# ScalarE takes the key's exponential first, and VectorE puts gate and key row between its two normalisations

## The chip, the cores and the metric

One core of one Trainium2 chip runs the whole program in one launch. The metric is the device time of that launch in microseconds (us). Five engines work side by side, each through an instruction list of its own, and meet at semaphores: TensorE (PE, with its weight loads shown as PEld), VectorE (DVE), ScalarE (ACT), GpSimd (POOL) and SyncE (SP), which issues transfers.

## The reference, cut to what matters

A pre-norm block: attention, then a mixture of experts. The change is in the attention part, which for each of 8 sequences of 512 tokens, 16 query heads and 4 key heads adds a causal softmax attention and a gated linear attention:

```python
q, k, v = x @ Wq, x @ Wk, x @ Wv                  # 16 / 4 / 4 heads of 128; g = k
qs = softmax(q, axis=-1); ks = softmax(k, axis=-1)  # over the 128 features of a head
gl = log_sigmoid(k) / 16.0
sq, sk = rotary(q), rotary(k)
# linear part, a scan over tokens:
S = S * exp(g_t)[..., None] + k_t[..., None] * v_t[..., None, :]   # k_t from ks, g_t from gl
o_gla = einsum('bhk,bhkv->bhv', q_t, S)                            # q_t from qs
# softmax part:
y = softmax(causal(sq @ sk.T * D ** -0.5)) @ v
out = (0.5 * y + 0.5 * o_gla) @ Wo
```

## The kernel before

The attention phase works in units: one unit is one key head with its four query heads of one sequence, so there are 32. While a unit c is attended, the features of unit c + 1 are prepared, in the same instruction lists. A unit has four steps s = 0 to 3. In step s each engine does, interleaved and in an order written out by hand:

- for the attended unit, head s: the scores of its four query blocks i = 3, 2, 1, 0, each with a row maximum (`row_max`, DVE), an exponential with row sum (`exponent`, ACT), a normalisation (`normalise`: a reciprocal of the row sum and a multiplication of `prob`, DVE), a transposition on PE (`turn_probs`), and the copy of the transposed blocks to `prob_t` (`past` on ACT, `diagonal` on DVE); then PE's `attend` and ACT's two output copies (`out_copy`), whose low part POOL makes (`out_low`). Scores, maxima, exponentials and normalisations of blocks 3 and 2 of head s + 1 are already done in step s.
- for the prepared unit, token tile a (a counts all 128 tiles, s is the tile within a unit): ACT takes the products from PSUM (`take_products`), the gate's exponential and logarithm (`gates`), and the feature exponentials of four queries and one key with their sums (`feature_exps`). DVE takes the feature maxima (`feature_max`), the rotary cosines (`rope_cosines`), the gate (`gate_logs`), and in `soften_keys` one reciprocal over all five sums and the multiplication of the key's row. POOL takes the rotary sines (`rope_sines`), the rotation in two instructions (`rotate`, L296 and L297), and the multiplication of the four query rows (`soften_queries`, L302), which waits for that reciprocal; then `out_low` (L337).
- one step later, for tile a - 1: PE transposes rotated keys, key rows and gate (`turn_features`, which waits for the rotation, the softened key and the gate), rotated queries (`turn_queries`), then blocks 2 of the probabilities, makes the next products, and goes on with `linear` (L892: query rows, L898: the state's update, which waits for POOL's `key_rest`, L332) and `chunk_local`. DVE copies the keys (`decays`, L625) after the normalisation of block 0; POOL's `differences` (L313) waits for that copy, ACT's exponential of the differences (L470) for POOL, and DVE's `apply_decays` (L641) for both ACT and PE's L892.

On DVE the end of step s and the start of step s + 1 read, before the change: `keep_local`, `normalise(s + 1, 3)`, `normalise(s + 1, 2)`, `gate_logs`, `soften_keys`, in the third unit of a sequence `x_low` (the next sequence's input, for which PE's `turn_features` waits in one step), in the second `statistics`; then `diagonal(3)`, `row_max(1)`, `normalise(1)`, `diagonal(2)`, `row_max(0)`, `normalise(0)`, `decays`. In step 3 there are no normalisations of a following head.

`gate`, `qk`, `logs`, `soft`, `prob` and `inv_tot` all lie in SBUF.

Of the kernel before, what the change touches and what calls it, by code (L numbers as in the profile page):

```python
# [20 lines left out]
G = HEADS // KV  # L21
# [3 lines left out]
NT = SEQ // P  # L25
# [16 lines left out]
def attention_phase(nc, x, w_q, w_k, w_v, w_o, consts, x2, acc, rows):  # L42
# [3 lines left out]
    with ExitStack() as ctx:  # L46
        def sb(name, shape, dt=F32):
            return ctx.enter_context(nc.sbuf_tensor(name, shape, dt))

        def sem(name):  # L50
            return ctx.enter_context(nc.semaphore(name))
# [30 lines left out]
        tot = sb("tot", [P, G + 1])  # L82
        inv_tot = sb("inv_tot", [P, G + 1])
# [50 lines left out]
        gate_ready = sem("gate_ready")  # L134
        qk_ready = sem("qk_ready")
        val_ready = sem("val_ready")
        exps_ready = sem("exps_ready")
        inv_ready = sem("inv_ready")
        rot_ready = sem("rot_ready")
# [79 lines left out]
        def block_index(c, h, i):  # L219
            return G * NT * c + NT * h + NT - 1 - i  # L220

        def use_index(c, h, i):

            return G * NT // 2 * c + NT // 2 * h + (NT - 1 - i) // 2
# [152 lines left out]
        def _(act):  # L377
# [71 lines left out]
            def feature_exps(a, ua, i):  # L449
                act.wait_ge(tops_ready, a + 1)  # L450
                act.wait_ge(soft_turned, a)
                act.wait_ge(k_rest_ready, (NT - 1) * ua + min(i, NT - 1))
                for h in range(G + 1):
                    ins = nc.scalar.activation(soft[:, h * DH:(h + 1) * DH], qk[:, h * DH:(h + 1) * DH], ACT.Exp,  # L454
                                               bias=neg_top[:, h:h + 1], accum_out=tot[:, h:h + 1])
                ins.then_inc(exps_ready, 1)

            def turned(a, ua, p, i):
# [54 lines left out]
        def _(dve):  # L513
# [58 lines left out]
            def row_max(c, h, i):  # L572
                n, j, w = block_index(c, h, i), NT * h + i, P * (i + 1)
                dve.wait_ge(scores_done, n + 1)
                nc.vector.tensor_reduce(neg_max[:, j:j + 1], score_ps[i % 2][:, 0:w], AX_X, ALU.max,  # L575
                                        negate=True).then_inc(max_ready, 1)

            def normalise(c, h, i):
                n, j, w = block_index(c, h, i), NT * h + i, P * (i + 1)
                dve.wait_ge(exp_ready[i % 2], use_index(c, h, i) + 1)  # L580
                nc.vector.reciprocal(inv_sum[:, j:j + 1], row_sum[:, j:j + 1]).then_inc(inv_sum_ready, 1)  # L581
                dve.wait_ge(inv_sum_ready, n + 1)
                nc.vector.tensor_scalar(prob[:, i % 2, 0:w], prob[:, i % 2, 0:w], inv_sum[:, j:j + 1], None,  # L583
                                        ALU.mult).then_inc(prob_ready, 1)

            def diagonal(c, h, i, p):

                dve.wait_ge(prob_turned[i % 2], use_index(c, h, i) + 1)
                dve.wait_ge(attended, G * c + h)
                dve.wait_ge(local_ready, NT * c + i + 1)  # L590
                nc.vector.tensor_tensor(prob_t[:, i, i * P:(i + 1) * P], prob_ps[i % 2][:, i * P:(i + 1) * P],  # L591
                                        local[p][:, i, h, :], ALU.add).then_inc(diag_ready, 1)

            def feature_max(a):
                dve.wait_ge(qk_ready, a + 1)
                dve.wait_ge(exps_ready, a)
                nc.vector.tensor_reduce(neg_top[:], qk[:].rearrange("p (h d) -> p h d", d=DH), AX_X, ALU.max,  # L597
                                        negate=True).then_inc(tops_ready, 1)
# [12 lines left out]
                nc.vector.scalar_tensor_tensor(out=gate[:], in0=qk[:, G * DH:QK], scalar=0.0, in1=logs[:],  # L611
                                               op0=ALU.min, op1=ALU.subtract).then_inc(gate_ready, 1)

            def soften_keys(a):
                dve.wait_ge(exps_ready, a + 1)
                dve.wait_ge(soft_query_ready, a)
                nc.vector.reciprocal(inv_tot[:], tot[:]).then_inc(inv_ready, 1)  # L617
                dve.wait_ge(inv_ready, a + 1)
                nc.vector.tensor_tensor(soft[:, G * DH:QK], soft[:, G * DH:QK], inv_tot[:, G:G + 1].to_broadcast([P, DH]),
                                        ALU.mult).then_inc(soft_key_ready, 1)  # L620

            def decays(a):
                dve.wait_ge(keys_turned, a + 1)
                dve.wait_ge(k_dec_ready, a)
                nc.vector.tensor_copy(keys[:], tr_ps[0][:, P:3 * P]).then_inc(keys_copied, 1)  # L625

            def turned_low(a, i, p):
                t = slice(i * P, (i + 1) * P)
                dve.wait_ge(kr_high_ready, a + 1)
                nc.vector.scalar_tensor_tensor(out=kr_t[p][:, 1, t], in0=tr_ps[0][:, 0:P], scalar=float(DH) ** -0.5,  # L630
                                               in1=kr_t[p][:, 0, t], op0=ALU.mult, op1=ALU.subtract).then_inc(kr_t_ready, 1)
                dve.wait_ge(qr_high_ready, a + 1)
                nc.vector.tensor_tensor(qr_t[p][:, 1, :, t], tr_ps[1][:].rearrange("p (h t) -> p h t", t=P),
                                        qr_t[p][:, 0, :, t], ALU.subtract).then_inc(qr_t_ready, 1)
# [41 lines left out]
            def unit(c, b, g, prepare, more):  # L676
                ua, p = (0, 0) if c is None else (c + 1, (g + 1) % 2)
                if prepare and c is not None:
                    dve.wait_ge(attended, G * c)
                if c is not None:  # L680
                    row_max(c, 0, 3)
                    row_max(c, 0, 2)
                if c is not None:
                    normalise(c, 0, 3)
                    normalise(c, 0, 2)
                for s in range(NT):
                    if c is not None:
                        diagonal(c, s, 3, g % 2)
                        row_max(c, s, 1)
                        normalise(c, s, 1)  # L690
                        diagonal(c, s, 2, g % 2)
                        row_max(c, s, 0)
                        normalise(c, s, 0)
                    if prepare and s:
                        decays(NT * ua + s - 1)
                        turned_low(NT * ua + s - 1, s - 1, p)
                        apply_decays(NT * ua + s - 1, ua, s - 1, p)
                    if c is not None:
                        if s < G - 1:
                            row_max(c, s + 1, 3)  # L700
                            row_max(c, s + 1, 2)
                        diagonal(c, s, 1, g % 2)
                        diagonal(c, s, 0, g % 2)
                    if prepare:
                        feature_max(NT * ua + s)
                        rope_cosines(NT * ua + s, s, 0 if c is None else G * c + s)
                    if c is not None and g and s == 0:
                        residual(c - 1, b, g - 1, PROJECTION[3:], tr_ps[1])
                    if prepare and s:
                        keep_local(NT * ua + s - 1, s - 1, p)  # L710
                    if c is not None and s < G - 1:
                        normalise(c, s + 1, 3)
                        normalise(c, s + 1, 2)
                    if prepare:
                        gate_logs(NT * ua + s)
                        soften_keys(NT * ua + s)
                    if more and g == KV - 2:
                        x_low(b + 1, s, tr_ps[min(s, 1)])
                    if more and g == KV - 3:
                        statistics(b + 1, s)  # L720
                        if s == NT - 1:
                            variances(b + 1)
                    if c is None:
                        split_low(STAGES + s)
                if prepare:
                    decays(NT * ua + NT - 1)
                    turned_low(NT * ua + NT - 1, NT - 1, p)
                if c is not None:
                    residual(c, b, g, PROJECTION[:2])
                if prepare:  # L730
                    apply_decays(NT * ua + NT - 1, ua, NT - 1, p)
                if c is not None:
                    residual(c, b, g, PROJECTION[2:3])
                if prepare:
                    keep_local(NT * ua + NT - 1, NT - 1, p)
                if more and g == KV - 3:
                    refine(b + 1)
                if c is not None and g == KV - 1:
                    residual(c, b, g, PROJECTION[3:])
# [1257 lines left out]
```

## Time and profile before

| | |
|---|---|
| median of 3 runs | 2831.75 us (2829.55 to 2834.02) |
| the profiled execution's own time | 2826.91 us |
| its span, first to last instruction | 2824.5 us |
| granted TensorE clock, mean | 0.97 |
| busy, PE / DVE / ACT / POOL | 90% / 69% / 55% / 55% |
| tiles prepared (steps), of them in units that also attend | 128, 124 |

Read the times of the profile against 2826.91 us, not against the median: the profiled execution is 4.84 us faster than the median. A timeline row gives start, duration, engine, line, operation, what is written from what, and in brackets how long the engine had been idle and what released it.

### The profile page before, as it was taken

The numbers are of one execution on the slowest core, as the hardware profiler recorded it, in microseconds if no ns is written. First come the engines' busy times: TensorE is split into PE (matmuls) and PEld (weight loads), VectorE is DVE, ScalarE is ACT, GpSimd is POOL, SyncE is SP. The second block draws the span as 40 slices with busy tenths as digits, with TensorE's granted clock in tenths as the row PEclk, the third lists the DMA queues.
The fourth block names the chain that finished last, engine by engine and source line by source line (L and its number), as shares of the span: only waits on it lengthen the run. The fifth ranks groups of instructions, "written<-read, shape, count | busy, mean of one in ns | idle before, by whom it ended". The sixth has DMA issues, their size and how long they took to land. (4 is left out here: it accounts for less than half of the span.)

```text
span 2824.5 us, 52828 instructions
## 1 busy us (share of the span) xinstructions
PE 2542.8 (90%) x16740; PEld 1728.0 (61%) x16740; DVE 1936.2 (69%) x4731; ACT 1553.6 (55%) x4655; POOL 1549.6 (55%) x2010
## 2 busy tenths in 40 slices
PE   3799999999999999999999999999975899978882
PEld 2566666666666666666666666666643355457761
DVE  5777767777776777777777767777745677647661
ACT  4566556656665566666566556656634243246661
POOL 3556556655655565565556456655511666646663
PEclk9899999999999999999999999999996999989996
DMA  4500000000000000000000000000002223249985
GB/s 171 189 1 16 3 29 1 16 31 1 2 16 31 1 16 31 2 1 16 31 1 16 8 25 1 2 31 1 1 17 93 99 68 122 86 144 257 271 223 148
DMA packets 65358, 156.80 MB, mean 56 GB/s; under 512 B 13367, under 2 KB 14647, under 8 KB 64256
## 3 DMA queue, kind: packets, MB, share of 16 engines
q1 hardware_dynamic: 48624, 132.91, 13.9%
q0 software_dynamic: 16384, 16.33, 3.2%
q10 hardware_dynamic: 80, 4.19, 0.4%
q8 instruction: 141, 2.31, 0.3%
q14 instruction: 129, 1.06, 0.1%
HBM read 120.31 MB, written 81.40 MB: 71 GB/s over the span
## 5 line engine op out<-in xcount | busy, mean ns | idle before, releaser
L412 ACT ACTIVATE prob<-score_ps,neg_max 128x512 f32<-128x512 f32 (+3 forms) x512 | 271.8, 531 | 276.1 <-DVE neg_max L575 246.6
L284 POOL TENSOR_TENSOR parts<-qk,rope 128x640 f32<-128x640 f32 x128 | 197.2, 1541 | 358.9 <-issue 302.3
L806 PE MATMUL out_ps<-prob_t,val 128*128 128x512 f32 (+3 forms) x1024 | 305.5, 441 | 26.0 <-ACT prob_t L418 24.0
L779 PE MATMUL score_ps<-kr_t,qr_t 128*128 128x512 f16 (+3 forms) x1536 | 284.8, 300 | 13.0 <-ACT prob L412 11.2
L583 DVE TENSOR_SCALAR prob<-prob,inv_sum 128x512 f32<-128x512 f32 (+3 forms) x512 | 273.5, 534 | 18.0
L806 PEld LDWEIGHTS out_ps<-prob_t,val 128*128 128x128 f32 x1024 | 185.1, 190 | 145.6 <-issue 62.4
L454 ACT ACTIVATE soft<-qk,neg_top 128x128 f32<-128x128 f32 x640 | 247.0, 387 | 5.6 <-DVE neg_top L597 2.1
L575 DVE TENSOR_REDUCE neg_max<-score_ps 128x1 f32<-128x512 f32 (+3 forms) x512 | 236.8, 482 | 7.2 <-PE score_ps L781 1.0
L313 POOL TENSOR_TENSOR decay<-keys 128x512 f32<-128x512 f32 x128 | 134.1, 1047 | 166.7 <-DVE keys L625 166.7
L852 PE MATMUL qkv_ps<-wq_high,x_t_high 128*128 128x512 f16 x512 | 195.8, 382 | 15.8 <-DVE wkv_low L523 15.8
L324 POOL TENSOR_TENSOR k_dec<-decay,keys 128x32 f32<-128x32 f32 (+3 forms) x512 | 165.3, 354 | 68.8 <-ACT decay L470 68.8
L581 DVE RECIPROCAL inv_sum<-row_sum 128x1 f32<-128x1 f32 x512 | 81.1, 158 | 174.6 <-ACT prob L412 174.6
L296 POOL TENSOR_TENSOR rot<-parts 128x320 f32<-128x320 f32 x128 | 110.7, 865 | 160.7 <-DVE parts L605 160.7
L852 PE MATMUL qkv_ps<-wq_low,x_t_high 128*128 128x512 f16 x512 | 195.5, 382 | 0.0
L852 PE MATMUL qkv_ps<-wq_high,x_t_low 128*128 128x512 f16 x512 | 195.2, 381 | 0.0
L337 POOL TENSOR_TENSOR o_t_low<-parts,o_t_high 128x512 f16<-128x512 f32 x128 | 147.9, 1155 | 74.8 <-ACT parts L428 74.8
L779 PEld LDWEIGHTS score_ps<-kr_t,qr_t 128*128 128x128 f16 x1536 | 135.7, 98 | 82.8 <-ACT prob L412 38.3
L302 POOL TENSOR_TENSOR soft<-soft,inv_tot 128x512 f32<-128x512 f32 x128 | 144.5, 1129 | 55.6 <-DVE inv_tot L617 55.6
L1761 POOL DMA_INDIRECT acc<-e_yo,e_goal x64 | 115.6, 1806 | 107.2 <-issue 89.3
L418 ACT COPY prob_t<-prob_ps 128x384 f32<-128x384 f32 (+1 forms) x256 | 94.2, 368 | 144.0 <-DVE prob_t L591 140.3
L1234 POOL DMA_INDIRECT rows<-r_yn,r_sk_i x128 | 129.0, 1008 | 53.9 <-issue 45.5
L470 ACT ACTIVATE decay<-decay 128x640 f32<-128x640 f32 x128 | 94.4, 738 | 93.4 <-POOL decay L316 93.4
(281 smaller groups left out, 7761.6 us busy)
## 6 DMA issues: line engine op xcount, KB each, us to landing
held_expert_w<-in_L_ffn_W_gate_dram SPq DMA_DIRECT2D x32, 512.0 KB, 5.0
held_expert_w<-in_L_ffn_W_up_dram SPq DMA_DIRECT2D x32, 512.0 KB, 6.8
held_expert_w<-in_L_ffn_W_down_dram SPq DMA_DIRECT2D x32, 512.0 KB, 7.7
rows<-const_empty_dram SPq DMA_DIRECT2D x1, 10560.0 KB, 39.4
e_xg<-rows SPq DMA_DIRECT2D x32, 330.0 KB, 4.5
x_in<-_attn_hidden_states_dram SPq DMA_DIRECT2D x8, 1024.0 KB, 5.4
x_acc<-_attn_hidden_states_dram SPq DMA_DIRECT2D x8, 1024.0 KB, 5.5
x<-x_acc SPq DMA_DIRECT2D x8, 1024.0 KB, 4.3
```

The costliest lines, as they stand in the source:

```text
L284: nc.gpsimd.tensor_tensor(parts[:, 1, :].rearrange("p (h d) -> p h d", d=HALF), qk[:].rearrange("p (h d) -> p h d", d=HALF), rope[:, i, 1: ...
L302: nc.gpsimd.tensor_tensor(q, q, inv_tot[:, 0:G].unsqueeze(2).to_broadcast([P, G, DH]), ALU.mult).then_inc(soft_query_ready, 1)
L313: nc.gpsimd.tensor_tensor(decay[:, 0:NSUB * P].rearrange("p (c s) -> p c s", s=P), mid.to_broadcast([P, NSUB, P]), run.unsqueeze(1).to_bro ...
L324: ins = nc.gpsimd.tensor_tensor(k_dec[:, s, 0:m], decay[:, s * P:s * P + m], keys[:, 0:m], ALU.mult)
L337: nc.gpsimd.tensor_tensor(o_t[1][:, h, :], o_whole, o_t[0][:, h, :], ALU.subtract).then_inc(o_t_ready, 1)
L412: nc.scalar.activation(prob[:, i % 2, 0:w], score_ps[i % 2][:, 0:w], ACT.Exp, bias=neg_max[:, j:j + 1], accum_out=row_sum[:, j:j + 1]).the ...
L454: ins = nc.scalar.activation(soft[:, h * DH:(h + 1) * DH], qk[:, h * DH:(h + 1) * DH], ACT.Exp, bias=neg_top[:, h:h + 1], accum_out=tot[:, ...
L575: nc.vector.tensor_reduce(neg_max[:, j:j + 1], score_ps[i % 2][:, 0:w], AX_X, ALU.max, negate=True).then_inc(max_ready, 1)
L583: nc.vector.tensor_scalar(prob[:, i % 2, 0:w], prob[:, i % 2, 0:w], inv_sum[:, j:j + 1], None, ALU.mult).then_inc(prob_ready, 1)
L779: nc.tensor.matmul(score_ps[i % 2][:, 0:w], qr_t[p][:, q_, h, i * P:(i + 1) * P], kr_t[p][:, k_, 0:w], start=(n == 0), stop=False)
L806: nc.tensor.matmul(out_ps[:, j * P:SEQ], val[p][:, j, :], prob_t[:, j, j * P:SEQ], start=(j == 0), stop=False, skip_group_check=True)
L852: ins = nc.tensor.matmul(qkv_ps[:, 0:G * DH], x_t[x_part][:, d, i * P:(i + 1) * P], wq[w][:, d, gn * G * DH:(gn + 1) * G * DH], start=(d = ...
```

## The change

ScalarE's loop over the five feature exponentials starts with the key (h = G) and raises a semaphore of its own after it. VectorE's `soften_keys` no longer takes one reciprocal over five sums: it waits for the key's exponential alone, takes the reciprocal of one sum and multiplies the key row. A new `query_totals` takes the reciprocal of the four query sums, which releases POOL's `soften_queries`. In the order of VectorE's list, gate and key row go between `normalise(s + 1, 3)` and `normalise(s + 1, 2)`, and `query_totals` behind `normalise(s + 1, 2)`.

```diff
@@ feature_exps (ScalarE)
-                for h in range(G + 1):
+                for h in (G, *range(G)):
                     ins = nc.scalar.activation(soft[:, h * DH:(h + 1) * DH], qk[:, h * DH:(h + 1) * DH], ACT.Exp,
                                                bias=neg_top[:, h:h + 1], accum_out=tot[:, h:h + 1])
+                    if h == G:
+                        ins.then_inc(key_exp_ready, 1)
                 ins.then_inc(exps_ready, 1)
@@ VectorE
-            def soften_keys(a):
+            def query_totals(a):
                 dve.wait_ge(exps_ready, a + 1)
                 dve.wait_ge(soft_query_ready, a)
-                nc.vector.reciprocal(inv_tot[:], tot[:]).then_inc(inv_ready, 1)
-                dve.wait_ge(inv_ready, a + 1)
+                nc.vector.reciprocal(inv_tot[:, 0:G], tot[:, 0:G]).then_inc(inv_ready, 1)
+
+            def soften_keys(a):
+                dve.wait_ge(key_exp_ready, a + 1)
+                nc.vector.reciprocal(inv_tot[:, G:G + 1], tot[:, G:G + 1]).then_inc(key_inv_ready, 1)
+                dve.wait_ge(key_inv_ready, a + 1)
                 nc.vector.tensor_tensor(soft[:, G * DH:QK], soft[:, G * DH:QK], inv_tot[:, G:G + 1].to_broadcast([P, DH]),
                                         ALU.mult).then_inc(soft_key_ready, 1)
@@ the unit's order (VectorE)
                     if c is not None and s < G - 1:
                         normalise(c, s + 1, 3)
-                        normalise(c, s + 1, 2)
                     if prepare:
                         gate_logs(NT * ua + s)
                         soften_keys(NT * ua + s)
+                    if c is not None and s < G - 1:
+                        normalise(c, s + 1, 2)
+                    if prepare:
+                        query_totals(NT * ua + s)
```

## Rows read from the trace of the kernel before

**Rows 1.** Busy time by stretch: engines, clock, DMA share, GB/s

```profile
700.00:1100.00 400.00, 389.74 (x2545) 270.88 (x2544) 294.35 (x764) 245.27 (x825) 237.39 (x313) 1.00 0.03 12
```

**Rows 2.** Waits, 300 to 1900 us: total, times, longest

```profile
PE tr_ps L870 <- DVE soft L619: 15.6, 63, 0.3
...
PE tr_ps L870 <- DVE x_t_low L557: 2.4, 6, 0.4
```

**Rows 3.** Timeline of all engines, end of step 1 of a first unit

```profile
1138.87 0.19 ACT L454 ACTIVATION_READ_ACCUMULATOR soft<-qk,neg_top 128x1 f32 x1
...
1139.51 0.52 DVE L583 TENSOR_SCALAR prob<-prob,inv_sum 128x512 f32<-128x512 f32 x1
...
1139.70 1.05 POOL L297 TENSOR_TENSOR rot<-parts 128x320 f32<-128x320 f32 x1
...
1139.95 0.15 DVE L581 RECIPROCAL inv_sum<-row_sum 128x1 f32<-128x1 f32 x1
...
1140.14 0.83 DVE L583 TENSOR_SCALAR prob<-prob,inv_sum 128x384 f32<-128x384 f32 x1
...
1140.89 0.28 DVE L611 SCALAR_TENSOR_TENSOR gate<-qk,logs 128x128 f32<-128x128 f32 x1
...
1141.10 0.18 DVE L617 RECIPROCAL inv_tot<-tot 128x5 f32<-128x5 f32 x1
...
1141.31 0.29 DVE L619 TENSOR_TENSOR soft<-soft,inv_tot 128x128 f32<-128x128 f32 x1
...
1141.35 1.14 POOL L302 TENSOR_TENSOR soft<-soft,inv_tot 128x512 f32<-128x512 f32 x1 [0.60 <-DVE inv_tot L617]
1141.52 0.28 DVE L591 TENSOR_TENSOR prob_t<-prob_ps,local 128x128 f32<-128x128 f32 x1
1141.70 0.30 PE L870 MATMUL tr_ps<-ident,rot 128*128 128x128 f32 x1 [0.17 <-DVE soft L619]
...
1142.46 1.16 POOL L337 TENSOR_TENSOR o_t_low<-parts,o_t_high 128x512 f16<-128x512 f32 x1
...
1142.81 0.16 DVE L581 RECIPROCAL inv_sum<-row_sum 128x1 f32<-128x1 f32 x1 [0.68 <-ACT prob L412]
...
1143.01 0.76 DVE L583 TENSOR_SCALAR prob<-prob,inv_sum 128x256 f32<-128x256 f32 x1
```

**Rows 4.** Timeline of VectorE and GpSimd in a step 3

```profile
1165.29 0.86 POOL L296 TENSOR_TENSOR rot<-parts 128x320 f32<-128x320 f32 x1 [0.79 <-DVE parts L605]
1165.73 0.57 DVE L611 SCALAR_TENSOR_TENSOR gate<-qk,logs 128x128 f32<-128x128 f32 x1
```

**Rows 5.** Timeline of VectorE, GpSimd idle meanwhile

```profile
1179.33 0.42 DVE L583 TENSOR_SCALAR prob<-prob,inv_sum 128x384 f32<-128x384 f32 x1
```

**Rows 6.** Timeline, step 2 of that unit

```profile
1147.28 0.46 POOL L332 TENSOR_TENSOR k_rest<-span,soft 128x128 f32<-128x128 f32 x1
1147.36 0.74 ACT L470 ACTIVATE decay<-decay 128x640 f32<-128x640 f32 x1 [0.46 <-POOL decay L316]
...
1148.13 0.69 DVE L641 TENSOR_TENSOR q_dec<-tr_ps,decay 128x512 f32<-128x512 f32 x1 [0.51 <-ACT decay L470]
...
1150.98 0.26 ACT L418 COPY prob_t<-prob_ps 128x128 f32<-128x128 f32 x1
...
1151.29 2.42 PE L806 MATMUL out_ps<-prob_t,val 128*128 128x512 f32 x8 [0.51 <-ACT prob_t L418]
```

**Rows 7.** Timeline, step 1 of that unit

```profile
1134.05 0.74 ACT L470 ACTIVATE decay<-decay 128x640 f32<-128x640 f32 x1 [0.46 <-POOL decay L316]
...
1134.97 0.69 DVE L641 TENSOR_TENSOR q_dec<-tr_ps,decay 128x512 f32<-128x512 f32 x1 [0.65 <-PE tr_ps L892]
```

**Rows 8.** Timeline of a second unit: VectorE with statistics

```profile
1190.87 0.69 DVE L528 BATCH_NORM_STATS2 bn<-x_in 128x6 f32<-128x512 f32 x1
...
1192.96 0.35 DVE L583 TENSOR_SCALAR prob<-prob,inv_sum 128x256 f32<-128x256 f32 x1
```

**Rows 9.** Timeline, step 3 of that unit

```profile
1160.82 0.46 POOL L332 TENSOR_TENSOR k_rest<-span,soft 128x128 f32<-128x128 f32 x1
...
1161.51 0.39 PE L898 MATMUL tr_ps<-val,k_rest 128*128 128x128 f32 x2
```

More of the change, by code:

```diff
@@ L136, in attention_phase @@
         val_ready = sem("val_ready")
+        key_exp_ready = sem("key_exp_ready")
+        key_inv_ready = sem("key_inv_ready")
         exps_ready = sem("exps_ready")
```

## The prediction

> **What bounds the kernel now.** I read busy time by stretch first. In the attention phase TensorE is busy 389.74 of 400 us at the full granted clock [rows 1], so at most 2.6% of that phase can be won by filling its gaps. Second, the waits: in 300 to 1900 us PE stands before `turn_features` 63 times for the softened key, 15.6 us in all, and 6 times for the next sequence's input [rows 2]. That is 0.25 us each. Third, the timelines, to see what stands behind each of these waits and how far the other engines are from binding.
>
> The steps repeat almost exactly, so one will do [rows 3]. VectorE normalises block 3 until 1140.03, starts block 2 at 1140.14 and ends it at 1140.97, has the gate at 1140.89, the reciprocal at 1141.10, the key row at 1141.31 to 1141.60, and `diagonal(3)` at 1141.52. PE begins at 1141.70 after 0.17 us of idle time. The key's row is thus late by some tenths, and VectorE has no idle time in this stretch.
>
> The reader is also to see who holds VectorE up. The multiplication of block 2 takes 0.83 us here, and 0.42 us where GpSimd is idle [rows 3, 5]. It ends 0.22 us after GpSimd's L297, which ends at 1140.75. The multiplication of block 1, 0.76 us long, ends at 1143.77, 0.15 us after the end of GpSimd's L337 at 1143.62 [rows 3]. The gate too, 0.28 us when GpSimd is idle, takes 0.57 us in a step 3: it ends at 1166.30, 0.15 us after L296 at 1166.15 [rows 3, 4]. So VectorE operations of these kinds, issued while GpSimd runs, finish only after GpSimd's instruction has ended.
>
> Further down the step a second loop nearly binds, and in one step of a unit does: VectorE's key copy, GpSimd's differences, ScalarE's exponential (ends 1148.10), VectorE at 1148.13 after 0.51 us of waiting for it; it ends in ScalarE's copy at 1150.98, for which PE's `attend` waits 0.51 us [rows 6].
>
> **The change, part by part.** *ScalarE.* The same five pairs in another order. A first pair ended 1139.06 [rows 3] and will be the key's; VectorE asks for it after 1139.95. No wait there, cost nothing. The cover is 0.9 us. In a step 3 the margin is smaller, but the key's pair still ends before the gate does.
>
> *VectorE, one more reciprocal.* In the rows the next instruction starts 0.21 us after a reciprocal of five [rows 3]. There are 128; 93 lie between two normalisations (31 units of three steps).
>
> *VectorE, the new order.* Here lies the price. The gate now stands where the second normalisation's reciprocal stood, at 1139.95, with L297 running until 1140.75. Its cost is bounded below by 0.28 us and above by waiting for L297 and 0.15 us more, end 1140.90 [rows 3, 4]. I take the upper: it is the case of rows 4, and what stood in this place, block 2, did wait. The old order spent this wait on a 0.42 us instruction that had only 0.22 us left to do after it; the new one spends it on the gate and has block 2 still to do. Then, with the spacings of rows 3: reciprocal of the key 1140.82, key row 1141.03 to 1141.32, reciprocal of block 2 at 1141.24, its multiplication 1141.43 to 1141.85 (0.42, GpSimd idle, [rows 5]), reciprocal of the query sums 1141.77, `diagonal(3)` 1141.97.
>
> So the key row is ready 0.28 us sooner, and PE's 0.17 us gap goes. But `diagonal(3)` comes 0.45 us later. L302, which started 0.25 us after its reciprocal [rows 3], starts at 1142.02 and not 1141.35: 0.67 us later, and L337 behind it ends at 1144.29.
>
> What is late next: the block 1 chain (copy, exponential, reciprocal) moves by 0.45 us, from 1142.81 to 1143.26. Its multiplication is issued at 1143.46, L337 having started at 1143.13, so it again waits for L337 and ends at 1144.44 against 1143.77: 0.67 us late. Behind it on VectorE stand `diagonal(2)`, `row_max(0)`, `normalise(0)` and the key copy, and for the copy wait GpSimd and ScalarE. All of that is 0.67 us late.
>
> A rule of the Trainium skill speaks against the change in the same way: "SBUF — State Buffer", section "Who interferes with whom", says that a Vector instruction with two SBUF inputs contends with a GpSimd instruction that reads SBUF, and that whichever issues first has the shared ports for the whole of its instruction. By it the moved gate, with both inputs in SBUF, is blocked; without it the sum would have the gate's 0.28 us. The 0.57 us gate of the trace agrees.
>
> **What of 0.67 us reaches PE.** After step 1 of a unit VectorE waits for ScalarE already, and PE for ScalarE [rows 6]: all of it, 0.66. After step 0 VectorE waits for PE's L892; ScalarE was done at 1134.79, 0.18 us before VectorE began at 1134.97 [rows 7], so some 0.15 us are slack: 0.51. After step 2 no scores follow, and PE has only the state's update to wait for: its operand was ready at 1161.28 and L898 ran at 1161.51 [rows 9]; less about 0.05 us for a semaphore that leaves 0.18 us of slack: 0.48. In step 3 and in the tail PE is the bound and hands the delay on. PE's earlier start of 0.2 us is lost before these waits. That is 1.65 us per unit in the first and fourth units of a sequence, 15 of them: 24.8 us.
>
> In the second units (8) the statistics stand before `diagonal(3)` [rows 8] and already pushed block 1 just past L337's end: 0.35 us, no wait. The new order moves it 0.45 us and L337's end 0.67 us, so it waits again, and ends some 0.48 us late. With the same slacks, smaller by what the wait took, I put 1.4 us per unit: 11 us. In the third units (8) PE waits in one step for the next input [rows 2], which moves by 0.45 us; the other two have more slack, and I estimate 0.23 us each: 0.9 us per unit, 7 us.
>
> Nothing in a step 3 changes the end: VectorE waits there for PE afterwards. In the four steps of the very first unit the key row now waits for L297, as it waited for the sums: nothing. Routing and experts are untouched.
>
> Sum: 24.8 + 11 + 7 = 43 us, on the execution's 2826.91: 2870. The median stands 4.84 us above it, so 2875 us.
>
> **The rivals.**
> *The gate slips in before L297.* L297 shows as started at 1139.70 but can only run once block 3 is done at 1140.03; the gate is issued just then. If it goes first, L297 ends about 0.15 us later, at 1140.90; the key row waits for that and ends 1141.05, block 2 ends 1141.57, `diagonal(3)` comes 0.16 us late and L302 0.38 us. By the same path about 0.8 us per unit in 15 units, 0.5 and 0.2 in the others: 18 us, 2850. For it: back-to-back issue; against it: GpSimd asked first.
> *It does what the order suggests: faster.* The gate is not held (0.28 us), the key row is ready at 1140.65, and block 2, issued at 1140.75 as L297 ends, takes 0.42 us; all of VectorE is 0.2 us ahead, and PE's gap before `turn_features` is gone: 15.6 us for 63 steps makes 19 us for the 78 such steps, 2812. It decides if the gate and key row each stay under 0.3 us there. Against it: rows 4.
> *Absorbed.* The delay lies in slack that the one step shown does not have: within 6 us of before. Against it: PE's `attend` waits, and VectorE before it [rows 6].
> *A new wait for the key's exponential* costs nothing by the 0.9 us above, and is no case.
>
> **How the numbers follow.** Forecast as summed: 0.62. Gate first: 0.16. Absorbed: 0.07. Faster: 0.15. A difference under 0.2% (6 us) can hardly be told from none. That makes slower 0.78, same 0.07, faster 0.15. The forecast's own range is from 2860 to 2890: all 93 steps at the full 0.67 us would be 62 us and 2894. The range reaches down past the second rival's 2850 and the absorbed case's upper side, and leaves the gain out: 2837 to 2890.
>
> **What would show it.** In the new trace: `gate` (one of two lengths) near 0.95 us in steps 0 to 2, ending 0.15 us after L297; block 2's multiplication at 0.42; PE idle before L870 for the softened key nearly nil in attending units; L302 0.67 us later against the gate's old place; PE's idle time before L898 and L806 grown to about 0.5 us or more; first and fourth units 1.65 us longer, second ones 1.4 us. The prediction is wrong if the gate stays at 0.28 us, or if block 1's multiplication isn't held by L337, which alone makes 0.45 into 0.67.

## The result, and the profile after

The changed kernel is slower: 2860.3 us median (2857.69 to 2870.37, 4 runs) against 2830.65 (2829.08 to 2834.02, 4 runs) on the same chip, ratio 1.0121 with a 95% interval of 1.0102 to 1.0141, that is 29 to 40 us, 34 by the ratio. The forecast was slower, with 2875 us and 2837 to 2890 as range: the direction and the mechanism are right, the size is too large, 43 us for 34 (2875 us lies 15 us above the median).

The profiled execution after has a span of 2855.3 us. The busy times from 300 to 1900 us of the kernel after, columns as in [rows 1] (after the length PE, PEld, DVE, ACT and POOL, then clock, DMA share and GB/s); TensorE's was 1551.31 us in the same stretch before, so it is busy 7 us less there.

```profile
300.00:1900.00 1600.00, 1544.08 (x9961) 1057.01 (x9961) 1188.77 (x3061) 957.78 (x3220) 901.59 (x1203) 1.00 0.04 12
```

The waits of the same stretch of the kernel after (engine and line, waited for: us in total, times, longest) show where TensorE and VectorE stand now. The wait for the softened key of [rows 2] is not in the list of what is over 3 us any more; in its place stands the state's update (L909, which was L898). VectorE's wait for ScalarE's exponential grew from 16.9 us (33 times) to 35.0 us (69 times):

```profile
DVE q_dec L649 <- ACT decay L474: 35.0, 69, 0.5
...
PE tr_ps L909 <- DVE qr_t L641: 20.8, 57, 0.4
```

The timeline of all engines at the end of step 1 of the same unit as [rows 3] shows the cause. L299 is the second rotation instruction, which was L297; L304 and L339 were L302 and L337.

```profile
1156.79 0.52 DVE L587 TENSOR_SCALAR prob<-prob,inv_sum 128x512 f32<-128x512 f32 x1
...
1156.99 1.04 POOL L299 TENSOR_TENSOR rot<-parts 128x320 f32<-128x320 f32 x1
...
1157.23 0.95 DVE L615 SCALAR_TENSOR_TENSOR gate<-qk,logs 128x128 f32<-128x128 f32 x1
...
1158.11 0.15 DVE L625 RECIPROCAL inv_tot<-tot 128x1 f32<-128x1 f32 x1
...
1158.29 0.29 DVE L627 TENSOR_TENSOR soft<-soft,inv_tot 128x128 f32<-128x128 f32 x1
...
1158.50 0.16 DVE L585 RECIPROCAL inv_sum<-row_sum 128x1 f32<-128x1 f32 x1
...
1158.68 0.30 PE L881 MATMUL tr_ps<-ident,rot 128*128 128x128 f32 x1
1158.69 0.42 DVE L587 TENSOR_SCALAR prob<-prob,inv_sum 128x384 f32<-128x384 f32 x1
...
1159.03 0.17 DVE L621 RECIPROCAL inv_tot<-tot 128x4 f32<-128x4 f32 x1
1159.11 0.26 DVE L595 TENSOR_TENSOR prob_t<-prob_ps,local 128x128 f32<-128x128 f32 x1
...
1159.28 1.04 POOL L304 TENSOR_TENSOR soft<-soft,inv_tot 128x512 f32<-128x512 f32 x1 [1.24 <-DVE inv_tot L621]
...
1160.27 1.16 POOL L339 TENSOR_TENSOR o_t_low<-parts,o_t_high 128x512 f16<-128x512 f32 x1
...
1160.58 0.99 DVE L587 TENSOR_SCALAR prob<-prob,inv_sum 128x256 f32<-128x256 f32 x1
```

The gate takes 0.95 us, where GpSimd's second rotation instruction holds it up. It is issued while the rotation runs and ends at 1158.18, 0.15 us after the rotation's end at 1158.03. Over all 128 gates the median is 948 ns, the least 278 ns. The key's transposition on PE (L881) has no idle time before it: the change does what it is for. But block 1's multiplication, 0.76 us in [rows 3], now takes 0.99 us and ends 0.14 us after L339. What follows, later in the step, answers to [rows 6]:

```profile
1164.15 0.27 PE L869 MATMUL qkv_ps<-wkv_high,x_t_low 128*128 128x256 f16 x1
...
1164.40 0.63 PE L903 MATMUL tr_ps<-ident,soft 128*128 128x128 f32 x4
...
1164.49 0.69 DVE L641 TENSOR_TENSOR qr_t<-tr_ps,qr_t 128x512 f16<-128x512 f32 x1 [0.19 <-ACT qr_t L471]
1164.84 0.45 POOL L334 TENSOR_TENSOR k_rest<-span,soft 128x128 f32<-128x128 f32 x1
1164.92 0.74 ACT L474 ACTIVATE decay<-decay 128x640 f32<-128x640 f32 x1 [0.46 <-POOL decay L318]
1165.40 0.46 PE L909 MATMUL tr_ps<-val,k_rest 128*128 128x128 f32 x2 [0.37 <-DVE qr_t L641]
1165.69 0.69 DVE L649 TENSOR_TENSOR q_dec<-tr_ps,decay 128x512 f32<-128x512 f32 x1 [0.51 <-ACT decay L474]
```

PE stands 0.37 us before the update, until VectorE's qr_t (1165.18) and GpSimd's k_rest (1165.29) are there. One gap of 0.2 to 0.3 us was closed and one of 0.37 us opened further down.

The idle times alone do not make up the loss, since matmuls overlap: in [rows 9]'s step one product begins 0.11 us after the other though each lasts 0.27. Counted from start to start, the update begins 1.25 us after the last product here (L869, 1164.15) and began 0.55 us after it before, as the timeline of the kernel before shows at [rows 9]:

```profile
1160.96 0.27 PE L858 MATMUL qkv_ps<-wkv_high,x_t_low 128*128 128x256 f16 x1
1161.07 0.60 PE L892 MATMUL tr_ps<-ident,soft 128*128 128x128 f32 x4
```

Of these 0.70 us, 0.14 lie before the query rows' transposition (L903, which was L892), which waits for VectorE's low part of the keys (L638, ends at 1164.30). The two matmuls of the update then take 0.08 us more, and the key's transposition follows its predecessor 0.30 us sooner than before. That leaves 0.47 us per step, in the medians of the first units' steps too.

Since the units repeat almost exactly, their length tells more than one execution's total. The table has the medians over the sequences, from the start of a unit's first gate to that of the next unit's first gate, in us, by the place of a unit in its sequence.

| kernel | first | second | third | fourth |
|---|---|---|---|---|
| before | 62.30 | 62.59 | 63.71 | 65.19 |
| after | 63.66 | 63.61 | 64.50 | 66.54 |
| old order | 62.88 | 62.88 | 63.74 | 65.79 |
| one-input gate | 62.43 | 62.42 | 63.31 | 65.35 |
| totals first | 64.24 | 65.97 | 66.90 | 67.13 |
| gate early | 62.50 | 63.23 | 64.34 | 65.83 |
| gate early, block 3 in its slot | 61.74 | 62.09 | 63.20 | 64.70 |
| the same, statistics in the wait | 61.74 | 62.31 | 63.21 | 64.70 |
| changed kernel, gate early | 62.50 | 62.54 | 63.41 | 65.46 |
| before, short low part | 62.29 | 62.62 | 63.52 | 65.21 |
| after, short low part | 61.71 | 63.48 | 64.39 | 64.62 |

After minus before: 1.36, 1.02, 0.79 and 1.35 us. With 15 first and fourth, 8 second and 8 third units that is 20.3 + 8.2 + 6.3 = 35 us, inside the measured 29 to 40. The two profiled executions differ by 30.8 us: 35.9 us more between the first gate and the last, and 4.8 us less behind the last, for which nothing here shows a cause.

### The profile page after: what moved, and what is told of

It reads as the page before. It is cut to its first block and busy times, and to the rows that moved or that the text cites. A ratio compares the mean times of both kernels' runs of the same rounds, so it can differ in the third digit from the quotient of the medians.

```text
span 2855.3 us, 52956 instructions
## 1 busy us (share of the span) xinstructions
PE 2568.1 (90%) x16740; PEld 1730.4 (61%) x16740; DVE 1988.5 (70%) x4859; ACT 1554.0 (54%) x4655; POOL 1536.6 (54%) x2010
## 5 line engine op out<-in xcount | busy, mean ns | idle before, releaser
L817 PE MATMUL out_ps<-prob_t,val 128*128 128x512 f32 (+3 forms) x1024 | 307.2, 443 | 24.9 <-ACT prob_t L420 22.8
L817 PEld LDWEIGHTS out_ps<-prob_t,val 128*128 128x128 f32 x1024 | 186.1, 191 | 145.1 <-issue 63.1
L587 DVE TENSOR_SCALAR prob<-prob,inv_sum 128x512 f32<-128x512 f32 (+3 forms) x512 | 240.6, 470 | 18.1
L304 POOL TENSOR_TENSOR soft<-soft,inv_tot 128x512 f32<-128x512 f32 x128 | 133.1, 1040 | 126.3 <-DVE inv_tot L621 126.3
L339 POOL TENSOR_TENSOR o_t_low<-parts,o_t_high 128x512 f16<-128x512 f32 x128 | 147.9, 1155 | 63.0 <-ACT parts L430 63.0
```

The lines of the kernel that those rows point to most:

```text
L304: nc.gpsimd.tensor_tensor(q, q, inv_tot[:, 0:G].unsqueeze(2).to_broadcast([P, G, DH]), ALU.mult).then_inc(soft_query_ready, 1)
L339: nc.gpsimd.tensor_tensor(o_t[1][:, h, :], o_whole, o_t[0][:, h, :], ALU.subtract).then_inc(o_t_ready, 1)
L817: nc.tensor.matmul(out_ps[:, j * P:SEQ], val[p][:, j, :], prob_t[:, j, j * P:SEQ], start=(j == 0), stop=False, skip_group_check=True)
```

## The experiments

The theory: an instruction of VectorE with two SBUF inputs, or a multiplication of `prob`, issued while a GpSimd instruction runs waits for its end, and the new order puts a short instruction into that wait and leaves the long one behind it. The rivals: the added reciprocal, ScalarE's order or the new semaphores, or the late query rows in themselves.

### Undoing the order alone

```diff
                     if c is not None and s < G - 1:
                         normalise(c, s + 1, 3)
+                        normalise(c, s + 1, 2)
                     if prepare:
                         gate_logs(NT * ua + s)
                         soften_keys(NT * ua + s)
-                    if c is not None and s < G - 1:
-                        normalise(c, s + 1, 2)
-                    if prepare:
                         query_totals(NT * ua + s)
```

> All of the change except the place of the instructions: the key's exponential first, two reciprocals, but both normalisations again ahead of gate, key row and query totals. Port theory (an instruction with two SBUF inputs issued while GpSimd runs is held until GpSimd's instruction ends): the gate is 0.28 us again, diagonal(3) some 0.07 us later than in the kernel before, the query rows on GpSimd 0.4 us later, block 1 held 0.3 us longer, of which 0.16 us is slack: +6 us, about 2836. Rival (the added reciprocal costs its 0.21 us in each of 93 steps): +20 us, about 2850. Rival (ScalarE's order or the new semaphores cost the 30 us): stays near 2860.

Measured: 2840.7 us, 1.0051 times the kernel before (1.0034 to 1.0068): 10 to 19 us, between the theory's 6 and the first rival's 20. The gate takes 0.28 us again. What is left of the loss has the predicted place and is larger than predicted, as the timeline of this kernel shows:

```profile
1150.56 0.28 DVE L615 SCALAR_TENSOR_TENSOR gate<-qk,logs 128x128 f32<-128x128 f32 x1
...
1151.15 0.17 DVE L621 RECIPROCAL inv_tot<-tot 128x4 f32<-128x4 f32 x1
1151.24 0.26 DVE L595 TENSOR_TENSOR prob_t<-prob_ps,local 128x128 f32<-128x128 f32 x1
...
1152.40 1.16 POOL L339 TENSOR_TENSOR o_t_low<-parts,o_t_high 128x512 f16<-128x512 f32 x1
...
1152.71 1.00 DVE L587 TENSOR_SCALAR prob<-prob,inv_sum 128x256 f32<-128x256 f32 x1
```

Block 1 ends 3.15 us after the gate's start and not 2.88 as in [rows 3]. The added reciprocal itself cost `diagonal(3)` only 0.05 us (0.68 after the gate, against 0.63): nothing waits for it, and the next instruction starts 0.09 us later. Through the later query rows, and L339 behind them, block 1 of first units ends 0.28 us late in each of three steps; that costs them 0.58 us, and all units together some 11 us by the table. So about a third of the loss (11 of 35 us by the table, 14 of 34 by the ratios) belongs to the split, by way of GpSimd, and the rest to the order.

### ScalarE's order alone

```diff
-                for h in range(G + 1):
+                for h in (G, *range(G)):
```

> The kernel before with ScalarE's order of the five exponentials changed alone. Both theories: VectorE waits for all five anyway: same as before within 0.2%, 2820 to 2836.

Measured: 2825.83 us, ratio 0.9996 (0.9986 to 1.0006). It costs nothing that can be told from zero (within 4 us).

### A gate that reads one SBUF tensor

```diff
-                nc.vector.scalar_tensor_tensor(out=gate[:], in0=qk[:, G * DH:QK], scalar=0.0, in1=logs[:],
-                                               op0=ALU.min, op1=ALU.subtract).then_inc(gate_ready, 1)
+                nc.vector.tensor_reduce(gate[:], logs[:].unsqueeze(2), AX_X, ALU.max,
+                                        negate=True).then_inc(gate_ready, 1)
```

> The changed kernel in its order, but the gate is written by an instruction that reads one SBUF tensor (it is the negative logarithm alone; the minimum with the key and the subtraction are left out). Port theory: this gate takes 0.28 us and not 0.95, the key row behind it is now the one that is held by the second rotation instruction (about 0.55 us), diagonal(3) comes 0.4 us sooner than in the changed kernel, and the time falls back to about 2830 (2822 to 2838). Rival (the order, the added reciprocal or the late query totals cost the time, not the held gate): stays at 2852 to 2860.

Measured: 2825.32 us, ratio 0.9999 (0.9990 to 1.0009). The order, both reciprocals and the late totals are all still there; the gate no longer reads a second tensor, and the whole loss is gone. This kernel leaves out the minimum with the key and the subtraction, so its results are wrong, and its gate is another operation as well: the run shows that the held gate costs the time, and by itself does not part the number of inputs from the kind of operation. The timeline of this kernel at the same place:

```profile
1152.52 1.05 POOL L299 TENSOR_TENSOR rot<-parts 128x320 f32<-128x320 f32 x1
1152.77 0.27 DVE L615 TENSOR_REDUCE gate<-logs 128x128 f32<-128x128 f32 x1
...
1153.14 0.57 DVE L627 TENSOR_TENSOR soft<-soft,inv_tot 128x128 f32<-128x128 f32 x1
1153.83 0.42 DVE L587 TENSOR_SCALAR prob<-prob,inv_sum 128x384 f32<-128x384 f32 x1
```

The gate is not held. The key row, with two SBUF inputs, now is, and ends at 1153.71, 0.14 us after the rotation at 1153.57. By the Trainium skill, "SBUF — State Buffer", section "Who interferes with whom", that is the dividing line: one SBUF input outside the two-port modes does not contend with GpSimd, two do where GpSimd's instruction reads SBUF. This trace agrees: 0.27 us for the gate, 0.57 us for the key row. The multiplication of `prob`, with one SBUF tensor and one factor per partition, is held too (0.83 us for 0.42); no run here tests why.

### Query totals ahead of block 2

```diff
                         gate_logs(NT * ua + s)
                         soften_keys(NT * ua + s)
+                        query_totals(NT * ua + s)
                     if c is not None and s < G - 1:
                         normalise(c, s + 1, 2)
-                    if prepare:
-                        query_totals(NT * ua + s)
```

> The changed kernel with the query totals ahead of normalise(s + 1, 2), so that GpSimd's query rows start at about the moment at which block 2's multiplication is issued. Port theory: if GpSimd's instruction is first, block 2 is held to its end, takes about 1.2 us and not 0.42, diagonal(3) comes 0.8 us later than in the changed kernel, and the time is about 2880; if VectorE is first by a few hundredths, the query rows and the low part behind them come 0.15 us sooner and the time is about 2852. Rival (a late start of the query rows is what costs): they start 0.45 us sooner here, so 2835 to 2845.

Measured: 2904.42 us, ratio 1.0277 (1.0262 to 1.0293), the worst of all although the query rows start 0.5 us sooner than in the changed kernel. So a late start of the query rows is not what makes up the loss; the run with the old order shows that it has a part in it. GpSimd came first, in the timeline of this kernel:

```profile
1183.13 1.04 POOL L304 TENSOR_TENSOR soft<-soft,inv_tot 128x512 f32<-128x512 f32 x1 [0.72 <-DVE inv_tot L621]
1183.13 1.25 DVE L587 TENSOR_SCALAR prob<-prob,inv_sum 128x384 f32<-128x384 f32 x1
```

Both show the same start; block 2 ends 0.21 us after GpSimd's instruction. The size was missed: 2880 was expected. Second and third units lose 2.4 us against the changed kernel, first and fourth 0.6. In all of them `diagonal(3)` comes 0.8 us later in each of three steps. In first and fourth units block 1 is then issued so late that the low part no longer holds it (0.35 us and not 1.00), which gives most of it back; in the others it was hardly held before (0.40 us).

### The gate moved forward, two ways

```diff
                         rope_cosines(NT * ua + s, s, 0 if c is None else G * c + s)
+                        gate_logs(NT * ua + s)
...
                     if prepare:
-                        gate_logs(NT * ua + s)
                         soften_keys(NT * ua + s)
```

> The kernel before with one move: the gate directly behind the rotary cosines, before GpSimd starts the rotation. Port theory: block 2's multiplication still ends 0.22 us after the second rotation instruction, so the 0.2 us of the gate vanish in a wait that VectorE has anyway; reciprocal, key row, query rows and diagonal(3) all come 0.2 us sooner, the gap before the key's transposition shrinks from 0.28 and 0.18 us to under 0.1, and the time is about 2813 (2808 to 2822). Rival (the gaps move elsewhere on TensorE): 2826 to 2834.

Measured: 2841.52 us, ratio 1.0056 (1.0044 to 1.0068): slower, where 17 us of gain were expected. The gate is at 0.28 us, as the theory has it, but it pushed block 3's multiplication past its slot between the two rotation instructions, in the timeline of this kernel:

```profile
1146.44 0.28 DVE L611 SCALAR_TENSOR_TENSOR gate<-qk,logs 128x128 f32<-128x128 f32 x1
...
1146.61 0.88 POOL L296 TENSOR_TENSOR rot<-parts 128x320 f32<-128x320 f32 x1 [1.22 <-DVE parts L605]
...
1147.43 0.87 POOL L297 TENSOR_TENSOR rot<-parts 128x320 f32<-128x320 f32 x1
1147.43 1.15 DVE L583 TENSOR_SCALAR prob<-prob,inv_sum 128x512 f32<-128x512 f32 x1
...
1148.64 0.66 PE L795 MATMUL prob_ps<-ident,prob 128*128 128x128 f32 x4 [0.21 <-DVE prob L583]
```

In [rows 3] it was issued at 1139.51, 0.19 us ahead of L297's start, and took 0.52 us. Here it is issued at the same moment as L297 and is held for the whole of it, while L297 takes 0.87 us and not 1.05; and PE waits for it. What the theory lacked was not the rule but this margin. The next kernel restores it: the reciprocal of block 3, which is not held, goes in front of `keep_local`, so that the multiplication follows `keep_local` at once.

```diff
                         gate_logs(NT * ua + s)
+                        if c is not None and s < G - 1:
+                            invert(c, s + 1, 3)          # the reciprocal half of normalise
...
-                        normalise(c, s + 1, 3)
+                        normalise(c, s + 1, 3, prepare)  # without it where it is done
```

> The kernel before with the gate behind the rotary cosines, as in the run before this, but with block 3's reciprocal ahead of keep_local, so that its multiplication is issued some 0.1 us sooner, ahead of GpSimd's second rotation instruction. Port theory: block 3 is again done between the two rotation instructions (0.5 us and not 1.15), the gate's 0.2 us vanish in block 2's wait for the second one, everything behind is 0.2 us sooner and TensorE's gap before the key's transposition shrinks: about 2812 (2806 to 2820). Rival (the gate so early costs in itself, whatever block 3 does): about 2840 again. Rival (TensorE's gaps only move): 2824 to 2832.

Measured: 2809.35 us, ratio 0.9937 (0.9924 to 0.9951): 14 to 21 us faster than the kernel before, and faster than both kernels of this case. Its timeline:

```profile
1131.73 0.48 DVE L588 TENSOR_SCALAR prob<-prob,inv_sum 128x512 f32<-128x512 f32 x1
1131.86 1.08 POOL L297 TENSOR_TENSOR rot<-parts 128x320 f32<-128x320 f32 x1
...
1132.32 0.83 DVE L588 TENSOR_SCALAR prob<-prob,inv_sum 128x384 f32<-128x384 f32 x1
```

Issued 0.13 us ahead of L297, block 3 takes 0.48 us. Block 2 still waits out L297 (0.83 us), and that wait has swallowed the gate's time.

### The changed kernel with the gate early

The same two edits on the changed kernel; its split and its order of key row, block 2 and totals stay.

> The changed kernel (key first, two reciprocals, key row ahead of block 2, totals last) with the gate moved early as in the faster version. Port theory: now the key row is the short two-input instruction that is held by the second rotation instruction and block 2 still has its 0.42 us behind it, as in the run with the one-input gate: about 2825 (2819 to 2832), some 15 us behind the faster version. Rival (only the gate's place was wrong, the rest of the change helps): 2809 or less.

Measured: 2829.85 us, ratio 1.0010 (1.0000 to 1.0019), in the expected range, and 20 us behind the faster version where 15 were expected. The short instruction that is held is now the key row, in its timeline:

```profile
1139.08 1.07 POOL L299 TENSOR_TENSOR rot<-parts 128x320 f32<-128x320 f32 x1
...
1139.54 0.76 DVE L632 TENSOR_TENSOR soft<-soft,inv_tot 128x128 f32<-128x128 f32 x1
...
1140.41 0.42 DVE L592 TENSOR_SCALAR prob<-prob,inv_sum 128x384 f32<-128x384 f32 x1
```

### Statistics in the wait

```diff
                         normalise(c, s + 1, 3, prepare)
+                        if more and g == KV - 3:
+                            statistics(b + 1, s)
```

The statistics of step 3 stay where they were.

> The faster version (gate early, block 3's reciprocal ahead of keep_local) with one more move, in second units alone: the statistics, which read one SBUF tensor, go between block 3's and block 2's multiplications, into VectorE's wait for the second rotation instruction. Port theory: there they are not held (0.69 us as before), block 2 ends about when it did, diagonal(3) of second units comes 0.4 us sooner, second units fall from 62.1 to about 61.75 us, 8 of them: 3 us less than the faster version, 2803 to 2809. Rival (anything put there costs its whole time): equal to the faster version or slower.

Measured: 2812.71 us, ratio 0.9957 (0.9943 to 0.9970), with second units at 62.31 us and not 62.09. A miss, which the timeline of a second unit explains:

```profile
1193.27 1.07 POOL L297 TENSOR_TENSOR rot<-parts 128x320 f32<-128x320 f32 x1
...
1193.54 0.69 DVE L528 BATCH_NORM_STATS2 bn<-x_in 128x6 f32<-128x512 f32 x1
...
1194.32 0.42 DVE L588 TENSOR_SCALAR prob<-prob,inv_sum 128x384 f32<-128x384 f32 x1
...
1195.27 0.30 PE L878 MATMUL tr_ps<-ident,rot 128*128 128x128 f32 x1 [0.18 <-issue]
...
1196.03 1.16 POOL L337 TENSOR_TENSOR o_t_low<-parts,o_t_high 128x512 f16<-128x512 f32 x1
...
1196.58 0.76 DVE L588 TENSOR_SCALAR prob<-prob,inv_sum 128x256 f32<-128x256 f32 x1
```

The statistics are not held (0.69 us), but they and block 2's reciprocal are longer than the wait they fill: block 2 ends at 1194.74, 0.40 us after L297 (1194.34) and not 0.22, the key row comes 0.18 us later, and PE stands 0.18 us before its transposition. `diagonal(3)` does come 0.43 us sooner, as expected, but nothing follows from it: block 1's multiplication, 0.35 us in the second units of the faster version, is now issued while L337 runs, takes 0.76 us, and ends 4.20 us after block 3's issue, as it did there.

### A short low part

```diff
-                nc.gpsimd.tensor_tensor(o_t[1][:, h, :], o_whole, o_t[0][:, h, :], ALU.subtract)
+                nc.gpsimd.tensor_tensor(o_t[1][:, h, 0:32], o_whole[:, 0:32], o_t[0][:, h, 0:32], ALU.subtract)
```

Once on the kernel before, once on the changed one; the rest of the low part is zero.

> The kernel before with out_low over 32 of 512 columns (15/16 of the low part of the attended output is left out), so that GpSimd is idle when block 1's multiplication is issued. Both theories: block 1 takes 0.35 us and not 0.75, 0.4 us more slack before TensorE's state update, but TensorE binds: 2818 to 2830. It is the base for the next run.

> The changed kernel with the same short out_low. Theory (the delay reaches TensorE because block 1, 0.3 us late, is then held by the low part to 0.54 us late, and 0.16 us of slack is all there is): block 1 ends 0.3 us later than in the run before, the slack there is 0.55 us, nothing of it reaches TensorE, and the gap before the key's transposition is gone: faster than the run before, by 0.2 us in most of 93 steps, 2803 to 2816. Rival (what costs is VectorE's longer way to diagonal(3) and the late query rows): slower than the run before by 15 us or more.

Measured: 2824.58 us, ratio 0.9990 (0.9981 to 0.9999), and 2828.34 us, ratio 1.0002 (0.9993 to 1.0012). The first is inside its range. The second is a miss for both sides: it is some 3 us slower than the first, where the theory had 2803 to 2816 us and the rival 15 us or more above the first. The units tell why. First and fourth units behave as the theory says: with the change they are 0.58 and 0.59 us shorter than without. Second and third units are 0.86 and 0.87 us longer. There the statistics or `x_low` stand on VectorE before `diagonal(3)`; block 1 is issued late enough to miss the low part (0.35 us with the short one, 0.35 to 0.40 with the full one), and `diagonal(3)` comes 0.29 us later in each of three steps: VectorE's own chain has no slack, and the whole of it arrives. So the low part is what costs in first and fourth units, some 20 of the 35 us; in the other units, some 15 us, it is VectorE's longer way to `diagonal(3)`, as the rival says. Both begin with the held gate. The timeline of a second unit of the changed kernel with the short low part shows it:

```profile
1199.61 0.46 PE L910 MATMUL tr_ps<-val,k_rest 128*128 128x128 f32 x2 [0.37 <-DVE qr_t L642]
```

## Why the prediction was right

*The gate is held by L297.* Right: 0.95 us in 93 steps, ending 0.15 us after the rotation. With another gate, which reads one tensor and is not held, the loss was gone. The rival in which the gate slips in before L297 is out, and so are the faster one and the absorbed one.

*The key row comes sooner, PE's gap goes.* Right. From the issue of block 3's multiplication the key row ended after 2.09 us before [rows 3] and 1.79 after.

*`diagonal(3)` 0.45 us late.* Mis-sized: 0.31 us (2.01 us after block 3's issue in [rows 3], 2.32 now). The term that failed is the reciprocal of the query totals, put at 0.21 us like the old one. The 0.21 us was the wait of the next instruction for its result; nothing waits for the new one on VectorE, and `diagonal(3)` starts 0.08 us after it.

*L302 0.67 us late, L337 behind it.* The start is right, 0.65 us. L337 ends only 0.53 us late, since the query rows now take 1.04 us and not 1.14, no longer beside VectorE's key row. So block 1 ends 0.52 us late and not 0.67. In second units `diagonal(3)` is 0.29 us late and block 1 0.35, where 0.45 and 0.48 were forecast; the hold by L339 adds 0.05 us there.

*What of it reaches PE.* Predicted 0.51, 0.66 and 0.48 us for the three steps; from gate to gate the steps before and after differ by 0.47, 0.38 and, with step 3, in which the gate keeps its place, 0.48 us in first units (medians of the gates' starts). The second is the larger miss. I took it that after step 1 there is no slack, from the 0.51 us wait of [rows 6]. That step was an odd one: its key copy started 0.24 us late for a reason that the profile does not show. In step 1 of 12 of the 15 first and fourth units VectorE waits for PE, as in step 0. This is one of them, from the timeline of the kernel before:

```profile
574.03 0.69 DVE L641 TENSOR_TENSOR q_dec<-tr_ps,decay 128x512 f32<-128x512 f32 x1 [0.65 <-PE tr_ps L892]
```

All three steps therefore have the slack of 0.15 us, and 0.52 less 0.15 is 0.37. That fits step 1, which ends in PE's wait for ScalarE before `attend`. The steps 0 and 2 go by PE's own gaps and not by that chain: 0.69 us more from the last product to the update, 0.08 more for its two matmuls, 0.30 less before the key's transposition, 0.47 in all. Two of the signs were missed with it. The gap before the update is 0.37 us and not 0.5 or more, and the one before `attend` (L806, now L817) did not grow: in step 1 of first units it is 0.52 us after and 0.60 before. In second units there was no slack to take off, as VectorE waits for ScalarE there already.

*The sum.* 1.65 us forecast and 1.36 measured in first and fourth units (20 us and not 25), 1.4 and 1.02 in second ones (8 and not 11), 0.9 and 0.79 in third ones (6 and not 7; step by step 0.30, 0.25 and 0.24 us for a forecast 0.45 and twice 0.23): 35 us for 43.

*Left open.* How far ahead of GpSimd an instruction of VectorE must be issued to go first. 0.13 us was enough for block 3, and 0.04 us for the key row, which in [rows 3] and in all 93 such steps of the kernel before is issued that much ahead of L302 and takes 0.29 us; 0.00 was not enough. Between 0.00 and 0.04 no run has anything. Why single steps start their key copy late was not tried either.

## What to carry to other kernels

Before moving a VectorE instruction, look at what GpSimd runs at its new place. In a wait for GpSimd put the longest instruction that is held anyway, which here paid only its last 0.15 to 0.3 us behind it, and not a short one in front of it; and move work that is not held only if it fits into what is left of the wait. A gap of TensorE closed at one wait is a gain only if the engines that feed the next wait are not made later. Price a loop from several of its rounds: one odd round gave half of the 0.28 us by which step 1 was missed here.

## What the runs showed of the hardware that was not expected

In these runs an instruction was either not held or held to the end of GpSimd's, and hundredths of a microsecond decided it. The same 128x512 multiplication took 0.48 us when issued 0.13 us ahead of GpSimd's instruction and 1.15 us when issued at the same moment; the two kernels differ by 32 us in all. The key row, issued 0.04 us ahead of the query rows, was not held (0.29 us); block 2, issued at the same moment as they were, was (1.25 us). And holding works both ways: GpSimd's query rows took 1.14 us beside VectorE's key row and 1.04 us without it, and its second rotation instruction 1.05 us where block 3 went first and 0.87 where it did not.
